# A graph kernel's edge sort: the destination part of the payload is multiplied on GpSimd in place of VectorE

## The reference

```
h = relu(layernorm(x)); x = x + L0(h)
h = relu(layernorm(x)); x = x + L1(h)
L0: h = x @ W_enc.T + b; two layers: m = W2 @ relu(W1 @ [h[src], h[dst]] + b1) + b2
    agg = segment_sum(m, dst); h = layernorm(h + W_upd @ [h, agg] + b); then W_out
L1: three layers: agg = mean over incoming edges of h[src]; h = agg @ Wl.T + bl + h @ Wr.T
```

## Time and profile before

| | |
|---|---|
| median of 3 runs | 4074.35 us (4071.66 to 4075.82) |
| the profiled execution | 4076.87 us, its span 4075.1 us |
| busy, share of the span | PE 85%, PEld 77%, DVE 72%, ACT 49%, POOL 26% |
| the sort, 39.90 to 612.00 us | DVE 530.80, PE 328.93, ACT 178.58, POOL 78.66 us busy of 572.10 |
| after 697 us (summing the edges and the layers) | PE 3080.88, DVE 2301.89 us busy of 3378.10 |

### The profile page before, as it was taken

How to read it: one execution, slowest core, us unless ns; L and a number is a source line. 1 busy time by engine, 2 the same in 40 slices (tenths; PEclk the granted TensorE clock), 3 DMA queues, 4 the chain that set the end, 5 groups by cost and what they waited for, 6 DMA issues and landing times.

```text
span 4075.1 us, 273319 instructions
## 1 busy us (share of the span) xinstructions
PE 3465.9 (85%) x109712; PEld 3135.7 (77%) x109712; DVE 2922.5 (72%) x8506; ACT 1979.8 (49%) x3687; POOL 1046.9 (26%) x1888
## 2 busy tenths in 40 slices
PE   3556565799999998699989999769999979998997
PEld 2444443799888887599978888658888879998996
DVE  5999998688666666688866666568888865556555
ACT  1233234355444445544444444466666655555554
POOL 1111113122222225422222222623333321121111
PEclk7777776899999999799999999779999989999999
DMA  3000002787666663477766666334444449967983
GB/s 61 7 6 6 6 5 69 206 218 220 199 186 186 193 187 83 105 215 215 215 180 191 182 192 181 66 93 149 148 149 148 148 139 276 273 200 212 272 276 112
DMA packets 456516, 629.11 MB, mean 154 GB/s; under 512 B 142108, under 2 KB 298260, under 8 KB 456433
## 3 DMA queue, kind: packets, MB, share of 16 engines
q1 hardware_dynamic: 422123, 597.49, 50.5%
q0 software_dynamic: 9600, 19.68, 2.6%
q10 hardware_dynamic: 24710, 10.93, 1.0%
HBM read 512.47 MB, written 115.42 MB: 154 GB/s over the span
## 4 chain that ended last, share of the span: by engine, by line
PE 72%; DVE 12%; issue 7%; ACT 3%; SPq 3%; DMA 1%; DVEq 1%; POOL 1%; ACTq 0%; POOLq 0%
PE psum L1176 24%; PE psum L1382 15%; PE psum L1369 10%; PE psum L1180 8%; PE psum L1194 8%; PE psum L1349 4%; DVE arena L867 1%; DVE AGGf L860 1%; DVE Hf L906 1%; PE psum L1357 1%; SPq L1039 1%; DVE Hf L854 1%; DVE AGGf L865 1%; PE psum L1581 1%; ACT AGGf L1788 1%
## 5 line engine op out<-in xcount | busy, mean ns | idle before, releaser
L1176 PE MATMUL psum<-tabf,arena 125*32 125x128 bf16 x60384 | 1416.3, 220 | 114.1 <-POOL arena L1109 53.9
L1176 PEld LDWEIGHTS psum<-tabf,arena 125*32 125x32 bf16 x60384 | 1237.8, 97 | 222.0 <-issue 148.1
L1180 PE MATMUL psum<-arena 96*32 96x128 bf16 x20928 | 1255.7, 222 | 35.9 <-issue 35.9
L1214 ACT ACTIVATE arena<-psum 128x512 f32<-128x512 f32 x1300 | 779.8, 600 | 983.1 <-PE psum L1180 980.7
L1180 PEld LDWEIGHTS psum<-arena 96*32 96x32 bf16 x20928 | 722.1, 96 | 61.8 <-issue 61.8
L1382 PE MATMUL psum<-tabr,cellr 125*125 125x256 f32 x5000 | 617.7, 283 | 35.8 <-DVE tabr L2024 35.8
L1382 PEld LDWEIGHTS psum<-tabr,cellr 125*125 125x125 f32 x5000 | 600.9, 187 | 36.2 <-issue 36.2
L1109 POOL COPY arena<-tabf 96x512 bf16<-96x512 bf16 x402 | 268.6, 669 | 1227.9 <-PE psum L1180 1169.9
L1231 DVE TENSOR_SCALAR arena<-arena,row 125x512 bf16<-125x512 bf16 x956 | 334.2, 350 | 322.3 <-PE psum L1180 268.5
L1194 PE MATMUL psum<-arena 128*32 128x129 f32 x10400 | 562.0, 277 | 2.0 <-issue 2.0
L1369 PE MATMUL psum<-tabf,arena 125*125 125x384 bf16 x2500 | 511.5, 327 | 0.0
(11 more groups left out here) (245 smaller groups left out, 4798.4 us busy)
## 6 DMA issues: line engine op xcount, KB each, us to landing
arena<-cells_kept SPq DMA_DIRECT2D x500, 315.0 KB
arena<-slots_turned SPq DMA_DIRECT2D x302, 384.0 KB
cells_kept<-arena SPq DMA_DIRECT2D x625, 126.0 KB
arena<-slots_turned SPq DMA_DIRECT2D x252, 288.0 KB
tabf<-slots_turned SPq DMA_DIRECT2D x100, 384.0 KB
arena<-slots_turned SPq DMA_DIRECT2D x50, 512.0 KB
tabf<-slots_turned SPq DMA_DIRECT2D x50, 512.0 KB
tabf<-rows_stacked SPq DMA_DIRECT2D x200, 96.0 KB
```

What stands on the lines that cost most here:

```text
L1176: pe.matmul(psCell[b][q:q + GW, g * D:(g + 1) * D], fr, rows, start=g == 0 and p == 0, stop=False, tile_position=(0, q), skip_group_check= ...
L1180: m = pe.matmul(psCell[b][q:q + GW, g * D:(g + 1) * D], toB[:, b, g * CELL + q:g * CELL + q + GW], cur[:, part_of(at), g, :], start=g == 0 ...
L1214: act.activation(msgs[:, SLOT[pos], :, 0:D], psCell[SLOT[pos]].rearrange("p (c d) -> p c d", d=D), ACT.Relu).then_inc(f_msg, 1)
```

## The change

The second multiply of the payload leaves `place` on VectorE and becomes `payload_destinations` on GpSimd, with the same operands. Two semaphores are new: `o_onek`, raised by VectorE when `one_k` is written, and `o_dest`, raised by GpSimd when the multiply is done. GpSimd's multiply of pair m waits for `o_onek` and, from the second pair on, for the fills of the pair before (`o_perm`), which read the payload. It stands in GpSimd's queue behind `starts` of pair m + 1, whose loop is written out anew for that. `fill` of the first tile of a pair waits for `o_dest`, since it reads the payload; VectorE waits for the `o_dest` of the pair before ahead of writing `one_k` (L887), and for that of an earlier pair ahead of `find_cells`, which overwrites `to2`. The wait before L893, on `o_dve` so far, is now on `o_onek`.

```diff
+            def payload_destinations(m, v, starting=False):
+                if not starting:
+                    hold(pool, "pool", o_perm, m * 2)
+                hold(pool, "pool", o_onek, m + 1)
+                pool.tensor_tensor(pairs(payload[:, :, KW:2 * KW]), pairs(one_k), along(to2[:, v], KW), ALU.mult).then_inc(o_dest, 1)
...
             starts(0, 0)
             prepare_weights()
-            with pool.Fori(0, SORTS // 2) as i:
+            starts(1, 1)
+            payload_destinations(0, 0, True)
+            with pool.Fori(0, SORTS // 2 - 1) as i:
                 step.enter(i, 2 * 5)
                 for k in range(2):
-                    starts(i * 2 + (k + 1), 1 - k)
-                step.leave(SORTS // 2)
+                    starts(i * 2 + (k + 2), k)
+                    payload_destinations(i * 2 + (k + 1), 1 - k)
+                step.leave(SORTS // 2 - 1)
+            starts(SORTS - 1, 0)
+            payload_destinations(SORTS - 2, 1)
+            payload_destinations(SORTS - 1, 0)
...
-            def fill(n, u, starting=False):
+            def fill(n, u, pair, starting=False):
                 pe.wait_ge(o_slot, n + 1)
+                if u == 0:
+                    pe.wait_ge(o_dest, pair + 1)
...
-            def find_cells(m, v, tiles):
+            def find_cells(m, v, tiles, level):
                 dve.wait_ge(o_win, m * (4 * RG * 16) + 4 * RG * 16)
+                if level > 1:
+                    dve.wait_ge(o_dest, m - 1)
...
-                c = step.did(dve.tensor_tensor(pairs(one_k), columns(col1, KW, BOTH), along(code2, KW), ALU.is_equal))
+                if not starting:
+                    dve.wait_ge(o_dest, m)
+                dve.tensor_tensor(pairs(one_k), columns(col1, KW, BOTH), along(code2, KW), ALU.is_equal).then_inc(o_onek, 1)
...
-                step.after(c)
+                dve.wait_ge(o_onek, m + 1)
                 step.did(dve.tensor_tensor(pairs(payload[:, :, 0:KW]), pairs(one_k), along(off2[:, v], KW), ALU.mult))
-                step.did(dve.tensor_tensor(pairs(payload[:, :, KW:2 * KW]), pairs(one_k), along(to2[:, v], KW), ALU.mult))
```

## The result

| | before | after |
|---|---|---|
| median | 4073.52 us (4 runs, 4071.66 to 4075.82) | 4104.6 us (4 runs, 4103.26 to 4105.11) |
| ratio | | 1.0078, 95% interval 1.0066 to 1.0091 |
| the profiled execution | 4076.87 us, span 4075.1 | 4104.62 us, span 4102.8 |

The median grew by 31 us, the profiled execution by 28, against a forecast of 39, to 4104.6 where 4113 was predicted. The time lies in the stated range of 4086 to 4144, and is slower by more than the 0.2% that a measurement can tell.

The account below looks back on a forecast made before the run. The prediction took VectorE's chain in the sort loop as the bound. Per pair, -0.65 saved, +2.15 hold and +0.05 waits give +1.55 us, times 25: +39, so 4113 us, with 4086 to 4144 for 8 in 10.

Parts of the forecast that it names:

- The bound, and where the time would go: Sort loop: VectorE, 93% busy, is the bound; changes to its chain count 25 times, once for each pair.
- The saving of 0.65 us: Without L894 on VectorE, the marks of L854 start 0.65 us earlier per pair, 16 us at most.
- The hold, +2.15 us a pair: A two-input VectorE operation among L891, L893 and L854 stands while GpSimd multiplies: 2.15 us a pair.
- the slope between two short records: GpSimd's two-input rate, from records of 128 and 512 elements: 1.81 to 2.05 ns an element.
- L1855's delay: VectorE's two-input L1855, issued behind GpSimd's L1929, was delayed 0.96 us; taken as the base of the hold.
- The waits, +0.05 us: Two more VectorE waits per pair, ahead of L887 and L817, already fulfilled: 0 to 0.1 us, taken as 0.05.
- The signs in the profile: L891, L893 or first L854 grows about 2.1 us; GpSimd record 2.2 to 3.3; period about 23.6; sort ends about 651.
- The sum: Per pair in the sort, -0.65 + 2.15 + 0.05 = +1.55 us, times 25: +39 us.
- That GpSimd doesn't hold VectorE up: In the payload step the two engines don't collide, so the 16 us are gained: 4058 us; chance 7%.
- the payload is late for TensorE: GpSimd's multiply ends after TensorE's L667 starts at 315.84, each pair growing by the excess: over 4200 us; chance 1%.
- the multiply is slow for its access pattern: GpSimd's payload multiply holds VectorE 3.4 us a pair, +70 us: 4144 us; chance 8%.
- This bf16 multiply is quicker than the rows with f32 inputs let one expect: GpSimd's payload multiply runs at the one-input rate, hold 0.92 us a pair, +8 us: 4082 us; chance 8%.

Follow-up runs that it names:

- the run with one multiply less: The kernel before without VectorE's source-offset multiply of the payload, its places cleared once at the start instead: 4060.62 us against 4075.54.
- The extra multiply: VectorE keeps both multiplies, with the change's semaphores; GpSimd also does the same multiply into an unread spare tile: 4119.98 us against 4074.7 for the kernel before.
- the extra copy: VectorE keeps both multiplies, with the change's semaphores; GpSimd also copies the one-hots into an unread spare tile: 3992.73 us against 3972.65 for the kernel before.
- the late run: The changed kernel with GpSimd's multiply released by VectorE's fold of the next pair's first ranks, beside the reduction: 4077.27 us against 4074.7 for the kernel before.

## Why the prediction was right, by its steps

**The bound, and where the time would go.** Right. The loss is 25 times the growth of a pair's period, in VectorE's chain; the stages behind the sort are shifted and otherwise the same.

**The saving of 0.65 us.** Right: the marks start 0.14 us after L914's end, and the run with one multiply less gained 15 us (11 to 21) where the prediction had 16.

**The hold, +2.15 us a pair.** The mechanism was right and this term was too large; it makes up the whole difference between the 39 us forecast and the 28 of the profiled execution. It is two errors in the same direction. First the rate: 1.70 ns an element, where the prediction went by the slope between two short records, 1.81 to 2.05, on top of L1855's delay; the hold is 1.90 us, not 2.15. (That delay of 0.96 us wasn't a whole hold either: L1855 was issued 0.15 us behind L1929, so up to 1.11 us. Counting that would have made the forecast larger still.) Second the place: GpSimd got in behind L914, and the first 0.14 us of its hold fell into the gap that VectorE had anyway, so that 1.68 came into the chain (0.08 of the difference to 1.90 the rows don't account for). I had named that gap and called it of little difference; it is worth 0.2 us a pair, 5 us in all. The extra multiply shows both cases: 1.90 where L916 stood back to back behind its forerunner, 1.67 where the marks behind the gap stood. So does the extra copy, 0.92 and 0.69, with the same 0.23 between them. So the growth was forecast 11 us too large by the spans; that the median lies only 8 us below 4113 owes some 3 us to luck, since the medians differ by 31.

**The waits, +0.05 us.** They were 0.07 to 0.10, which the range of 0 to 0.1 held.

**The signs in the profile.** Only the marks stood, and not L891 or L893; the record of GpSimd's multiply is 2.94 us, within the 2.2 to 3.3 that were named. The period is 23.21 us and not 23.6, and the sort ends 28.5 us later and not 39.

**The sum.** By what was measured: 25 x (-0.65 + 1.68 + 0.10) = 28 us, and the spans differ by 27.7. The medians of few runs differ by 31; the profiled execution before, 4076.87 us, was slower than each of the four runs behind its median.

**The rivals.** That GpSimd doesn't hold VectorE up, that the payload is late for TensorE, and that the multiply is slow for its access pattern are all gone. This bf16 multiply is quicker than the rows with f32 inputs let one expect, but by 6 to 17% (1.70 against 1.81 and 2.05 ns), not by half.

**What the prediction took from the Trainium skill.** The shutting out is as "SBUF — State Buffer", section "Who interferes with whom", has it. For its length, neither "the whole instruction" (2.94 us here, and 2.10 in the run where it waited for nothing) nor the 2.6 cycles an element that the Trainium skill gives in "GPSIMD Engine Reference", section 3.1, for f32 numbers, at its 1.2 GHz, are what was measured on these bf16 numbers: a hold of 1.90 us, or 1.70 x 1.2 = 2.0 cycles an element. The measurement decides.

## What to carry to other kernels

An idle GpSimd is not free help for a busy VectorE: what counts is not how long its operation takes but which VectorE operations stand while it reads. Price a move as the time saved on VectorE against the reading time on GpSimd, 1.7 ns an element for two bf16 inputs here, which is three times VectorE's own 0.58 (0.65 us for 1120); at equal work the move loses unless the reading falls beside reductions, waits or other operations that don't share the port. Where there is such a stretch, release the multiply so that GpSimd already stands waiting when the stretch begins, and cut it to fit.

## What I had not expected of the hardware

- GpSimd's record is longer than its hold on VectorE: of the 2.10 us of an undisturbed multiply VectorE is held for 1.90, and both in the change and in the late run it goes on 0.14 us before GpSimd's record ends. The earlier trace rows had it already: L1855 without its delay would have started at 693.13 - 0.68 = 692.45, 0.13 before L1929's end at 692.58.
- A one-input TENSOR_SCALAR of only 128x160 (int32 to f32) stands under a GpSimd multiply as a two-input operation does, 0.96 us in place of 0.24; the reduction ahead of it, of 128x1040 bf16, is not touched at all.
- Which VectorE operation stands isn't fixed. GpSimd, issued 0.02 us before L914's record began, got in behind it and not ahead of it, and with one more multiply in VectorE's queue it got in behind L915 in 16 pairs and behind L916 in nine (the delays of 1.90 and 1.67 us). Why the one or the other wasn't tried.
